# A linear attention's context, made per head into the two halves of the partitions instead of per pair of heads

## The reference, cut to what matters

```
q, k, v = split(layernorm(x) @ w_qkv)      # per head: 256 tokens x 64
q = softmax(q over the 64 features) * 64 ** -0.5
k = softmax(k over the 256 tokens)
context = k^T @ v                          # per head: 64 x 64
out = q @ context, heads side by side, @ w_out + b_out
x = x + out
```

## Time and profile before

| | |
|---|---|
| median of 3 runs | 1631.88 us (1629.13 to 1632.33) |
| profiled execution: span from first to last instruction | 1617.8 us |
| median less span | 14.1 us |
| TensorE busy | 1439.9 us (89%), 10746 matmul instructions |
| TensorE's weight loads | 725.6 us (45%) |
| VectorE, ScalarE, GpSimd busy | 992.2, 804.3, 455.9 us |
| mean granted TensorE clock | 0.954 |

### The profile page before, as it was taken

One profiled execution on the slowest core, in us unless ns is written; L12 is line 12 of the kernel. 1 busy time (PEld: TensorE's weight loads), 2 busy tenths in 40 slices (PEclk: granted clock), 3 DMA queues, 4 the chain that ended last, 5 costly groups with the idle time before them and its releaser, 6 DMA issues. The chain is left out here.

```text
span 1617.8 us, 30013 instructions
## 1 busy us (share of the span) xinstructions
PE 1439.9 (89%) x10746; PEld 725.6 (45%) x10746; DVE 992.2 (61%) x1940; ACT 804.3 (50%) x1498; POOL 455.9 (28%) x656
## 2 busy tenths in 40 slices
PE   7998899999999999878987899899977788978887
PEld 5777634444454443536653452222334333433354
DVE  5666488888163221364557759998376667356746
ACT  4455437677633332304541054777754456445647
POOL 7111220000003567240035430000021456134531
PEclk9999999999999999979997899999986989898999
DMA  2000263221110000001000055322000431143100
GB/s 102 1 0 0 98 203 100 54 51 30 52 69 1 1 0 0 1 1 46 18 7 1 0 161 169 100 54 50 20 13 9 167 100 50 37 167 101 51 2 27
DMA packets 82393, 85.45 MB, mean 53 GB/s; under 512 B 7244, under 2 KB 67916, under 8 KB 81772
## 3 DMA queue, kind: packets, MB, share of 16 engines
q1 hardware_dynamic: 82296, 84.18, 16.9%
HBM read 51.06 MB, written 32.51 MB: 52 GB/s over the span
## 5 line engine op out<-in xcount | busy, mean ns | idle before, releaser
L1335 ACT ACTIVATE arena<-ps 128x1024 f32<-128x1024 f32 x256 | 261.8, 1023 | 109.4 <-PE ps L1242 108.9
L1227 PE MATMUL ps<-k_stack,q_stack 49*128 49x512 bf16 x512 | 190.6, 382 | 14.5 <-DVE small L1358 12.1
L1242 PE MATMUL ps<-q_stack,k_stack 51*128 51x256 bf16 x1024 | 189.6, 272 | 0.6 <-ACT arena L1335 0.4
L1355 DVE CUSTOM_DVE_ANT_0 small<-ps,mask_b 128x512 bf16<-128x512 f32 x256 | 168.0, 689 | 29.6 <-PE ps L1227 28.1
L1358 DVE TENSOR_REDUCE small<-ps 128x1 f32<-128x512 f32 x256 | 162.0, 685 | 15.9 <-PE ps L1227 14.9
L1544 DVE TENSOR_REDUCE small<-ps 128x6 f32<-128x768 f32 x128 | 122.6, 958 | 76.3 <-PE ps L1424 73.8
L1254 PE MATMUL ps<-arena,v_pad 128*32 128x256 f32 x2048 | 162.4, 391 | 1.1 <-ACT arena L1335 1.1
L1521 ACT ACTIVATE arena<-ps 128x384 f32<-128x384 f32 x256 | 118.0, 488 | 78.4 <-PE ps L1446 77.7
L1132 POOL TENSOR_SCALAR_AFFINE_SELECT arena<-arena 128x256 f32<-128x256 f32 x256 | 101.8, 406 | 86.6 <-ACT arena L1521 86.3
L2602 DVE TENSOR_TENSOR arena<-ps,arena 128x512 f32<-128x512 f32 x64 | 44.3, 692 | 101.1 <-PE ps L2519 101.0
L2676 POOL TENSOR_TENSOR arena<-arena 128x512 f32<-128x512 f32 x64 | 79.7, 1266 | 94.3 <-ACT arena L2571 94.3
(11 more groups left out here) (357 smaller groups left out, 2983.7 us busy)
## 6 DMA issues: line engine op xcount, KB each, us to landing
q_stack<-q_scratch SPq DMA_DIRECT2D x128, 96.0 KB
k_stack<-k_scratch SPq DMA_DIRECT2D x64, 192.0 KB
k_scratch<-arena SPq DMA_DIRECT2D x8, 768.0 KB, 3.9
k_stack<-k_scratch SPq DMA_DIRECT2D x64, 96.0 KB
q_scratch<-arena SPq DMA_DIRECT2D x4, 1152.0 KB, 7.5
arena<-in_ctxT SPq DMA_DIRECT2D x8, 512.0 KB, 6.3
k_scratch<-arena SPq DMA_DIRECT2D x8, 512.0 KB, 4.7
k_scratch<-arena SPq DMA_DIRECT2D x16, 256.0 KB, 3.8
```

The costliest lines, as they stand in the source:

```text
L1227: pe.matmul(ps[:, t, :], c.q_stack[par][64 * e:64 * e + ROW_MAX, pr, t * P:(t + 1) * P], c.k_stack[par][64 * e:64 * e + ROW_MAX, pr, :], s ...
L1242: mm = pe.matmul(ps[:, bank, (ch % 2) * S:(ch % 2 + 1) * S], c.k_stack[prv][64 * e:64 * e + ROWS, pr, ch * P:(ch + 1) * P], c.q_stack[prv] ...
L1335: act.activation(buf.probs[i % 8], ps[:, bank:bank + 2, :].rearrange("p a n -> p (a n)"), ACT.Exp, scale=scale).then_inc(g["probs"].sem, 1)
L1355: dve.tensor_tensor_reduce(buf.junk[t], ps[:, t, :], c.mask_b[:, M_X + t * SC:M_X + (t + 1) * SC], 1.0, FLOOR, op0=ALU.add, op1=ALU.max, a ...
```

## The change

Each block j of two heads is now made by two products per half of the tokens (e = 0, 1): the 64 columns of one head of `ktok` as weights, the same head's 64 columns of `qtok` streamed, and the result written to the partitions 64 e to 64 e + 63 and the columns of the head's diagonal block. The off-diagonal blocks are no longer written, and nobody reads them. The order of everything else, the waits and the increments are as before; the program gives the first products a column tile of 64 at position 0, the second ones at position 64. `skip_group_check` concerns the program's builder alone.

```diff
                     for u in range(2):
                         for j in range(4):
-                            blk = slice((4 * u + j) * P, (4 * u + j + 1) * P)
                             for t in range(2):
-                                mm = pe.matmul(ps[:, 4 + u, j * P:(j + 1) * P], ktok[:, t, blk], qtok[prv][:, t, blk],
-                                               start=(t == 0), stop=(t == 1))
+                                for e in range(2):
+                                    at = (4 * u + j) * P + XDH * e
+                                    mm = pe.matmul(ps[XDH * e:XDH * (e + 1), 4 + u, j * P + XDH * e:j * P + XDH * (e + 1)],
+                                                   ktok[:, t, at:at + XDH], qtok[prv][:, t, at:at + XDH],
+                                                   start=(t == 0), stop=(t == 1), skip_group_check=True)
                         mm.then_inc(g["context"].sem, 1)
```

## The result

| | before | after |
|---|---|---|
| median of the runs | 1627.06 us (20 runs) | 1614.47 us (20 runs) |
| ratio after to before | | 0.9925 (0.9904 to 0.9945) |
| profiled execution's own time | | 1604.65 us |
| its span | 1617.8 us | 1602.9 us |
| its granted clock | 0.954 | 0.953 |

The gain is under 2%, but the interval of the ratio excludes 1. One run of the changed kernel (1632.24 us, at a granted clock of 0.935) counts as slow and is left out of the ratio.

The account below looks back on a forecast made before the run. The prediction took a ring through all engines, with the context as a link, to bound the step. Seven steady steps (11.0 us) and the last (1.8) save 12.8 us, from 1631.88 to 1619.1 us; range 1615.5 to 1626.

Parts of the forecast that it names:

- The ring: Steady step through all engines: the context, 3.67 us to q_proj(0), is a link, so the step follows its length.
- Load and stream equal, each hiding the other: Context pairs: loading 128 f32 columns costs as much as streaming them, 115 ns a pair; cutting only the stream gains nothing.
- Two halves at once: Context: pairs in the array's two column halves run together, 57 ns a round; 32 rounds and first load 1.88 us.
- Leaving the half mode: Between context and q_proj(0): 0.11 us in which nothing starts plus a bare full load of 0.11, together 0.22 us.
- A steady step: Seven steady steps: each saves 3.67 - (1.88 + 0.22) = 1.57 us, 11.0 us in all.
- The last step: Last context, 5.46 us, partly at the 1.2 GHz clock level: would take about 3.5 us; counted as 1.8 us saved.
- A sign that was wrongly set: Evidence to look for in the profile: the changed line's first and last start lie 7 x 1.57 us closer.
- 1 (halves in turn): Context: halves take turns or issue binds near 54 ns; 3.67 to 3.9 us, total 1632 to 1634; 0.10 with the clock rival.
- 2 (issue): Context: TensorE's sequencer can't issue the doubled instructions, 65 ns a pair, 5.7 us slower, 1637.6; chance 0.05.
- 3 (clock): Granted clock falls in or behind each new context, taking back 11.4 of 12.8 us, 1630.5; 0.10 together with halves in turn.
- 4 (not on the ring): Context: if q_proj(0) were not waited for, nothing would be gained; called excluded for all but a fraction, no separate chance.
- The step that failed: Whole time: 14.1 us between profiled span and three-run median 1631.88 kept unchanged, taking span 1605.0 to 1619.1 us.

Follow-up runs that it names:

- e6: Changed kernel with only the load halved: 64 weight columns into each half, 128 streamed; context to q_proj(0) 3.65 us, step 18.80 us.
- e7: Changed kernel with only the stream halved: 128 weight columns at full width, 64 streamed; context to q_proj(0) 7.19 us, step 22.30 us.
- r2: Kernel before, with q_proj(0) ahead of the context and q's maximum and subtraction ahead of L671; step 17.44 us, median 1617.11 us, ratio 0.9968.
- e5: Changed kernel, context alternating block by block: j = 0 and 2 in halves, 1 and 3 at full width; context to q_proj(0) 4.00 us, step 19.05 us.
- r1: Changed kernel, with q_proj(0) ahead of the context and q's maximum and subtraction ahead of L671; step 16.72 us, median 1612.59 us, ratio 0.9929 to before.
- e1: Changed kernel with both heads' products written to partitions 0 to 63, the same half of the array; context to q_proj(0) 3.87 us, step 19.02 us.
- e3: Changed kernel with, for each bank, all 16 pairs of head 0's half, then 16 of head 1's; context to q_proj(0) 3.34 us, step 18.51 us.
- e2: Changed kernel with e outside t in each block, so four passes' pairs in a row go to one half; context to q_proj(0) 2.06 us, step 17.22 us.
- a_again: The changed kernel once more, on the same chip as r1 and r2; step 17.17 us, median 1610.94 us (12 runs), ratio to before 0.9926.

## Why the prediction was right or wrong

- **The ring: right.** The context's length goes into the step one to one, in nine kernels from 2.01 to 7.19 us.
- **Load and stream equal, each hiding the other: right**, by e6 and e7 from both sides. The 115 ns for each old pair were not "both at once with a little between": in r2, where the context follows q_proj(0) without a wait, 32 pairs take 62.37 - 58.80 = 3.57 us, 112 ns each. The other 0.10 us of 3.67 were the first load, bare behind the wait.
- **Two halves at once: right.** A round is 58 ns (57 forecast), 32 of them 1.87 us. The Trainium skill's rule that loads overlap only where the row group differs (TensorE: Matmul & The Clock Gate, The mechanism) would by itself have left no gain here. The same section also lets a load into the background weight buffer go ahead of matmuls in flight, which the forecast left out. Against the rule taken by itself speak the change's 2.01 us, L1894's 54 ns, and at full width e7's 112 ns a pair, where load and stream one after the other would be 103 + 54 ns.
- **Leaving the half mode: right in kind, 0.18 instead of 0.22 us**, 0.08 of gap and 0.10 of load. "Entering costs nothing that shows" holds for the change, where TensorE waits before the context anyway. Where it does not wait, entering costs about 0.15 us (e5), and r1's context starts 62.56 - 60.75 = 1.81 us behind q_proj(0), r2's 1.72.
- **A steady step: 1.55 us, forecast 1.57. The last step: 1.71 us of the change's own**, forecast 1.8; the way to it (a fall of the clock that would be there again) was wrong, so that its 1.8 came so near is in part luck. This execution had no fall in the last step, and one at 32 us instead. The step's working is also not closed: 5.46 less 3.5 is 1.96, not 1.8.
- **A sign that was wrongly set.** The line's first and last start were to lie 7 x 1.57 = 11.0 us closer. They lie 14.2 us closer (36.1 to 172.2 before, 36.7 to 158.6 after), as the last start stands inside the last context, which itself became 3.4 us shorter (5.46 to 2.09).
- **Rivals.** 1 (halves in turn) is what e1 built: 3.87 us, inside the priced 3.67 to 3.9. 2 (issue) is out: 64 pairs in 1.9 us are 29 ns each, about half of the 62 ns that the Trainium skill gives in the section named there (TensorE: Matmul & The Clock Gate, Wait — 56ns, not 53.3ns?). 3 (clock): 1.00 in all steady steps. 4 (not on the ring) is out, by the table of nine kernels.
- **The step that failed: "The median of the runs, 1631.88, lies 14.1 above that span, for what lies around it; I leave those as they are".** This put the level of before, the term from which the 12.8 us are taken, about 5 us too high. A run's time lies 1.75 us above its span (1604.65 - 1602.9), not 14.1. The other 12.3 us were the distance between one execution, with a granted clock of 0.954, and the median of three others. Twenty runs put the median at 1627.06; from there the same 12.8 us give 1614.3, against 1614.47. The range was made from the costs of the edit alone (3.6 us down and 6.9 up) and held nothing of the level, although three runs can't fix a median among runs that spread over 22 us. I had read their spread of 3.2 us as the measurement's. With a level that may as well be 5 us lower, as it was, the range had to begin near 1611.

## What to carry to other kernels

A block-diagonal product of two 64-wide heads can be made as two products in the two column halves of the array, for half the time, if load and stream shrink together and neighbouring instructions go to different halves (four in a row to one half cost 0.05 us; sixteen in a row lose 1.33 of the 1.86 us that lie between the change and e1). Stay in one mode: each change costs 0.15 to 0.19 us, so a context of 32 small rounds can pay for one. A single block can't: in e5 it gains 4 x (0.112 - 0.058) = 0.22 us in halves, and entering and leaving cost 0.34. When the level of a forecast is taken from a few runs, look at how the time of a run hangs on its granted clock first; differences inside a step of the profile are read to 0.05 us, where the medians of twenty runs leave 3 open.

## What the runs showed of the hardware

- TensorE starts small pairs faster than any long run in the profile of before: 64 in 1.9 us, 29 ns each, load included.
- It starts pairs past others that wait for their half of the array: three at each border in e3, and with runs of four pairs (e2) only 0.05 us are lost.
- The granted clock falls at different places in executions of the same kernel. The change's first profile has 1.00 from 36 us on up to 667 us. In a_again, the same program, it is 0.51 again from 174.7 to 178.1 us. Over the twenty runs of the change the time goes from 1604.55 us at a clock of 0.953 to 1632.24 at 0.935.
